# Loads moved between two DMA queues in one stage, and transfers cut by columns instead of by partitions in another

## The chip, the cores and the metric

The kernel runs on one core of a Trainium2 chip. The metric is the device time of one execution in microseconds (us). The engines are TensorE (PE in the profile, PEld for its weight loads), VectorE (DVE), ScalarE (ACT), GpSimd (POOL) and SyncE (SP). SP and POOL each issue DMA transfers in the order of their programs: an instruction that waits for a semaphore holds back everything behind it on that engine.

## The reference

Two transformer-like layers on x of 2 x 4096 tokens with 256 features, all in float32. Only the first attention of the first layer is touched by the change:

```python
h = layernorm(x) * (1 + ca) + sa
q, k, v = ...                       # 16 heads of 16; q and k normalised
def step(state, (q_t, k_t, v_t, a_t, b_t)):
    state = a_t * state
    delta = b_t * (v_t - state @ k_t)
    state = state + outer(delta, k_t)
    return state, state @ q_t       # one output per token
out = rms_norm(outs) * rms_w * silu(h @ Wgate)
x = x + ga * (out @ Wout)
```

The later parts (a token-choice feed-forward of 32 experts, a windowed attention, a mixture of 8 experts) are the same before and after.

## The kernel before

The recurrence is computed in chunks of 16 tokens. Three stages stand in a row, each with its own block of instructions for every engine and a barrier at its end.

**Chunk stage** (`build_delta_chunks`). 64 tiles of 128 tokens go through a software pipeline of 102 iterations. Phase A projects a tile and stores `rows` (v, k, q, gate), `small` and the products of pairs of tokens (`pairs_q`, `pairs_k`) to HBM. Phase B takes a group of 16 tiles, spread over 16 iterations: it reads the pairs back as two tiles `kk` and `qkd` of 128 partitions x 4096 numbers, one partition for each chunk (16 KB in a row), weighs them with decays, inverts the triangular systems in `kk` on DVE (`eliminate`), and stores the results as `inverse` and `qkd`. Phase C reads `inverse` back tile by tile (`load_inverse`), with `c_rows` and `c_fac`, ACT makes `blocks` of it, PE solves, and `vw` is stored. There are four groups. Each load and each store of `kk` and `qkd` goes in `PIECES = 4` pieces of 512 KB; piece i holds the partitions 32 i to 32 i + 31 (`lines_of`). Since a tile of tokens is 8 partitions of the group, four tiles of a group lie in one piece, and `load_inverse` waits for the one piece that holds its tile (`inverse_out[piece]`). SP issues all loads, POOL all stores.

**State scan** (`build_state_scan`): untouched.

**Output stage** (`build_delta_outputs`). 32 pairs of tiles. For pair m PE multiplies `u` by blocks (`mix`, L1300), DVE adds `read` (`add`, L1402), ACT squares, DVE reduces, ACT takes the root, DVE normalises and multiplies by the gate (L1419, signal `o_ready`), PE turns (L1310) and projects (L1319), and DVE adds the result to x (`add_x`, L1427, signal `x_ready`), from where POOL stores it as `x1`. In iteration m of DVE's program stand `add(m)`, `normalize(m)` and `add_x(m - 2)`, in that order; ACT's iteration m ends, where m % 4 is 1, with `silu(m // 4 + 1)` of the gate rows of the next four pairs. PE's order is `mix(m)`, `turn(m - 1)`, `project(m - 2)`. Buffers: two `u` of a pair (256 KB), two `read`, `qkd` and `x` of four tiles (512 KB), two `gate` of eight tiles (1 MB). All loads are SP's, in one order: `load_qkd`, `load_u`, `load_read`, and behind them at every fourth pair `load_gate` (waits for `o_ready` of the pair that last read the buffer) and at every second `load_x` (waits until the store of the buffer's old x has landed).

Of the kernel before, what the change touches and what calls it, by code (L numbers as in the profile page):

```python
# [10 lines left out]
BATCH, SEQ, DIM = 2, 4096, 256  # L11
# [83 lines left out]
def chunk_rows(dram, g):  # L95

    return dram.rearrange("(g p t) f -> g p (t f)", g=GROUPS, p=P)[bass.ds(g, 1)].rearrange("a p f -> (a p) f")
# [152 lines left out]
def build_delta_chunks(nc, d, gamma_last):  # L250
# [6 lines left out]
    PIECES = 4  # L257
    LINES = P // PIECES
    C_ROWS, C_SMALL, OUTS = 8, 4, 4
# [4 lines left out]
    with ExitStack() as ctx:  # L264
# [65 lines left out]
        fac_out, qkd_out = map(sem.from_zero, ("fac_out", "qkd_out"))  # L330
        inverse_out = [sem.from_zero(f"inverse_out{piece}") for piece in range(PIECES)]
        c_in = [sem(f"c_in{i}") for i in range(C_ROWS)]
# [4 lines left out]

        def lines_of(piece):
            return slice(piece * LINES, (piece + 1) * LINES)

# [6 lines left out]
        with nc.Block() as block:  # L347
            @block.sync
            def _(sync):
# [11 lines left out]
                def load_keys(g, piece):  # L361
                    if piece == 0:
                        for i in both:
                            sync.wait_ge(pairs_out[i], 32 * TILES_OF_GROUP // 4 * (g + 1))
                        if g > 0:
                            for out_of in inverse_out:
                                sync.wait_ge(out_of, 16 * g)
                    sync.dma_start(kk[lines_of(piece), :], chunk_rows(d["pairs_k"], g)[lines_of(piece), :]).then_inc(kk_in, 16)

                def load_queries(g, piece):  # L370
                    if piece == 0 and g > 0:
                        sync.wait_ge(qkd_out, 16 * PIECES * g)
                    sync.dma_start(qkd[lines_of(piece), :], chunk_rows(d["pairs_q"], g)[lines_of(piece), :]).then_inc(qkd_in, 16)

# [9 lines left out]
                def load_inverse(c):  # L384
                    g, m = divmod(c, TILES_OF_GROUP)
                    if c >= C_SMALL:
                        sync.wait_ge(blocks_ready, at(c - C_SMALL + 1))
                    sync.wait_ge(inverse_out[m * PIECES // TILES_OF_GROUP], 16 * (g + 1))
                    sync.dma_start(inverse[c % C_SMALL][:, :, :].rearrange("p h t -> p (h t)"), tile_rows(d["inverse"], c)).then_inc(inverse_in[c % C_SMALL], 16)
# [32 lines left out]
            def _(pool):  # L422
# [13 lines left out]
                for n in range(ITERATIONS):  # L436
# [8 lines left out]
                    if m == TILES_OF_GROUP - 3:  # L445
                        pool.wait_ge(solved, at(g + 1))
                        for piece in range(PIECES):
                            pool.dma_start(chunk_rows(d["inverse"], g)[lines_of(piece), :], kk[lines_of(piece), :]).then_inc(inverse_out[piece], 16)
                    for piece in range(PIECES):
                        g, m = group_at(n - piece)  # L450
                        if m == TILES_OF_GROUP - 1:
                            pool.wait_ge(qkd_ready, at(g + 1))
                            pool.dma_start(chunk_rows(d["qkd"], g)[lines_of(piece), :], qkd[lines_of(piece), :]).then_inc(qkd_out, 16)
                    c = n - C_LAG - 1
# [722 lines left out]
def build_delta_outputs(nc, d):  # L1177
# [5 lines left out]
    BATCH_PAIRS = PAIRS_OF_TILES // BATCH  # L1183
    EIGHTS = TILES // 8
    with ExitStack() as ctx:
        sb = lambda name, shape: ctx.enter_context(nc.sbuf_tensor("do_" + name, shape, F32))
# [12 lines left out]
        gate = [sb(f"gate{i}", [P, 8, DIM]) for i in both]  # L1199
        x = [sb(f"x{i}", [P, Q, DIM]) for i in both]  # L1200
        o = [sb(f"o{i}", [P, 2, DIM]) for i in both]
# [9 lines left out]
        turned, oT_ready, projected, x_ready, begun = map(sem, ("turned", "oT_ready", "projected", "x_ready", "begun"))  # L1211
        u_in, qkd_in, read_in, gate_in, x_in = ([sem(f"{n}{i}") for i in both] for n in ("u_in", "qkd_in", "read_in", "gate_in", "x_in"))
        x_out = [sem.from_zero(f"x_out{i}") for i in both]
        CONSTS = 16 * (3 + BATCH)
# [10 lines left out]
        with nc.Block() as block:  # L1225
            @block.sync
            def _(sync):
# [14 lines left out]

                def load_gate(e):
                    if e >= 2:
                        sync.wait_ge(o_ready, at((e - 1) * 4))
                    sync.dma_start(gate[e % 2][:, :, :], tiles_of(d["rows"], e, 8)[:, :, 3 * DIM:4 * DIM]).then_inc(gate_in[e % 2], 16)

                def load_x(q):
                    if q >= 2:
                        sync.wait_ge(x_out[q % 2], q // 2 * 16)  # L1250
                    sync.dma_start(x[q % 2][:, :, :], tiles_of(d["x"], q, Q)).then_inc(x_in[q % 2], 16)

                sync.dma_start(parity[:, :], d["parity"]).then_inc(parity_in, 16)
# [3 lines left out]
                load_read(0)  # L1257
                load_gate(0)
                sync.dma_start(w_out[:, :, :], d["w_out"].rearrange("(k p) n -> p k n", p=P)).then_inc(consts, 16)
# [5 lines left out]
                load_read(1)  # L1265
                load_x(0)
                load_x(1)
                load_gate(1)
                for m in range(2, PAIRS_OF_TILES):
                    if m % 2 == 0 and m // 2 + 1 < QUADS:  # L1270
                        load_qkd(m // 2 + 1)
                    load_u(m)
                    if m % 2 == 1 and m // 2 + 1 < QUADS:
                        load_read(m // 2 + 1)
                    if m % 4 == 3 and m // 4 + 2 < EIGHTS:
                        load_gate(m // 4 + 2)
                    if m % 2 == 1 and m >= 5 and m // 2 < QUADS:
                        load_x(m // 2)

            @block.gpsimd  # L1280
            def _(pool):
                for q in range(QUADS):
                    pool.wait_ge(x_ready, at((q + 1) * 2))
                    pool.dma_start(tiles_of(d["x1"], q, Q), x[q % 2][:, :, :]).then_inc(x_out[q % 2], 16)
                for i in both:
                    pool.wait_ge(x_out[i], QUADS // 2 * 16)

# [50 lines left out]
            def _(act):  # L1338
# [20 lines left out]
                def silu(e):  # L1359
                    act.wait_ge(gate_in[e % 2], at((e // 2 + 1) * 16))  # L1360
                    act.activation(gate[e % 2][:, :, :], gate[e % 2][:, :, :], ACT.Silu).then_inc(silued, 1)
# [23 lines left out]
            def _(vec):  # L1385
# [35 lines left out]
                def add_x(m):  # L1421
                    q, half = divmod(m, 2)
                    vec.wait_ge(projected, at(m + 1))
                    if half == 0:
                        vec.wait_ge(x_in[q % 2], at((q // 2 + 1) * 16))
                    rows = flat_pair(x[q % 2], half)
                    vec.tensor_tensor(rows, rows, y_ps[m % 2][:, :, :].rearrange("p n f -> p (n f)"), ALU.add).then_inc(x_ready, 1)  # L1427
# [1594 lines left out]
```

## Time and profile before

| | us |
|---|---|
| median of 3 runs (3786.72 to 3790.21) | 3787.32 |
| the profiled execution | 3794.78 |
| its span, first to last instruction | 3793.0 |
| chunk stage in it, about 40 to 778 | 738 |
| output stage in it, about 1309 to 1620 | 311 |

The profile is of one execution. The profiled execution's own time is 1.8 us above its span and 7.5 us above the median. Times in the rows below count from the first instruction of the span. Because the stages are separated by barriers, time that a stage loses or gains moves all later stages by the same amount.

### The profile page before, as it was taken

The page shows a single profiled execution, that of the slowest core. Times are in us where ns is not written, and L with a number is a line of the kernel's source. Part 1 is how long each engine was busy: PE and PEld are TensorE (multiplying, and loading weights), DVE is VectorE, ACT ScalarE, POOL GpSimd, SP SyncE. Part 2 cuts the span into 40 slices and gives each one's busy share as a digit, 9 for nine tenths or more (in the row PEclk, how much of TensorE's full clock was granted, in tenths as well). Part 3 has the DMA queues.
Part 4 walks back from the last instruction along what each step waited for, and adds up shares of the span by engine and source line. Part 5 has one row for each costly group of instructions (what it writes and reads, how often), then busy time and mean ns, then how long its engine had stood idle before and what let it go on. Part 6 is the DMA issues. An engine that isn't in the chain of part 4 may idle for free. (4 is left out here: it accounts for less than half of the span.)

```text
span 3793.0 us, 108279 instructions
## 1 busy us (share of the span) xinstructions
PE 2521.0 (66%) x42132; PEld 1857.3 (49%) x42132; DVE 2027.5 (53%) x5459; ACT 1309.6 (35%) x3125; POOL 791.6 (21%) x1161
## 2 busy tenths in 40 slices
PE   5987883468888565755762887777760049999900
PEld 2554553445555354622441565555540049999800
DVE  2386887646666343464023677766763024444476
ACT  3766663346666433331000343333330012222200
POOL 0222221125555400000000110010103630000076
PEclk8998995555555577776765888888865579999955
DMA  3458888834444454524957211111114322222275
GB/s 105 162 183 257 263 277 275 275 101 102 100 100 103 104 161 146 174 99 164 414 232 285 97 59 58 58 58 58 58 46 145 105 79 69 72 69 71 64 224 162
DMA packets 387346, 534.51 MB, mean 141 GB/s; under 512 B 122140, under 2 KB 315640, under 8 KB 379384
## 3 DMA queue, kind: packets, MB, share of 16 engines
q1 hardware_dynamic: 308184, 343.88, 28.4%
q0 software_dynamic: 58688, 152.42, 12.8%
q10 hardware_dynamic: 20320, 36.44, 2.6%
q8 instruction: 61, 1.00, 0.1%
q14 instruction: 93, 0.76, 0.1%
HBM read 327.58 MB, written 216.15 MB: 143 GB/s over the span
## 5 line engine op out<-in xcount | busy, mean ns | idle before, releaser
L1108 ACT ACTIVATE ss_write_ps<-ss_state,ss_gammas 128x64 f32<-128x64 f32 x1024 | 263.3, 303 | 196.9 <-DVE ss_state L1156 196.9
L479 PE MATMUL dc_rows_ps<-dc_weights,dc_hT 128*128 128x512 f32 x512 | 264.0, 640 | 20.0 <-ACT dc_rows L608 17.4
L2728 PE MATMUL se_up_ps<-se_xT,se_w 128*128 128x128 f32 x2176 | 266.3, 276 | 0.1
L2736 PE MATMUL se_y_ps<-se_w,se_aT 128*128 128x256 f32 x1088 | 257.2, 379 | 0.0
L2728 PEld LDWEIGHTS se_up_ps<-se_xT,se_w 128*128 128x128 f32 x2176 | 254.8, 193 | 0.5 <-DVE se_w L2793 0.5
L2866 POOL DMA_INDIRECT cb_y<-scratch_ys,cb_to x128 | 137.3, 1073 | 564.1 <-DVE cb_to L2880 525.4
L2793 DVE COPY se_w<-mx_weights 128x2048 f32 x136 | 166.7, 1227 | 101.5 <-issue 101.5
L2736 PEld LDWEIGHTS se_y_ps<-se_w,se_aT 128*128 128x128 f32 x1088 | 196.4, 190 | 21.1
L1073 PE MATMUL ss_write_ps<-ss_solved,ss_k_rows 16*64 16x64 f32 x4096 | 180.7, 322 | 38.2 <-DVE ss_solved L1151 37.9
L1156 DVE TENSOR_TENSOR ss_state<-ss_write_ps,ss_block_mask 128x128 f32<-128x128 f32 x512 | 129.5, 291 | 135.7 <-PE ss_write_ps L1073 135.7
L2718 PE MATMUL se_xt_ps<-se_ident,se_xs 128*128 128x128 f32 x272 | 52.2, 275 | 223.0 <-DMA se_xs<-scratch_xs 223.0
L2763 ACT COPY se_xT<-se_xt_ps 128x256 f32<-128x256 f32 x136 | 50.6, 372 | 412.8 <-PE se_xt_ps L2718 412.8
L1030 POOL DMA_DIRECT2D scratch_solved_u<-ss_solved x256 | 135.4, 529 | 251.5 <-DVE ss_solved L1151 229.5
L1064 PE MATMUL ss_read_ps<-ss_state,ss_wq 128*32 128x64 f32 x4096 | 168.0, 314 | 26.3 <-DVE ss_state L1156 25.3
L1073 PEld LDWEIGHTS ss_write_ps<-ss_solved,ss_k_rows 16*64 16x64 f32 x4096 | 136.7, 208 | 93.9 <-ACT ss_write_ps L1108 62.0
L2799 DVE COPY se_y<-se_y_ps 128x256 f32<-128x256 f32 x136 | 57.7, 424 | 214.6 <-PE se_y_ps L2736 214.6
L1300 PE MATMUL do_mix_ps<-do_u,do_blocks 32*32 32x16 f32 x8192 | 89.0, 189 | 121.0 <-DMA do_u<-scratch_solved_u 73.5
L2288 POOL TENSOR_TENSOR wa_exps<-wa_exps,wa_nears 128x192 f32<-128x192 f32 x64 | 38.7, 605 | 594.9 <-ACT wa_one L2233 594.9
L2647 POOL DMA_INDIRECT scratch_xs<-dp_h,dp_to x128 | 125.8, 983 | 140.1 <-issue 115.6
L2718 PEld LDWEIGHTS se_xt_ps<-se_ident,se_xs 128*128 128x128 f32 x272 | 38.3, 142 | 238.1 <-DMA se_ident<-in_ident 224.5
L1300 PEld LDWEIGHTS do_mix_ps<-do_u,do_blocks 32*32 32x32 f32 x8192 | 85.2, 118 | 133.8 <-issue 133.8
L2768 ACT ACTIVATE se_aT<-se_up_ps 128x512 f32<-128x512 f32 x136 | 81.2, 597 | 196.2 <-PE se_up_ps L2728 196.2
(350 smaller groups left out, 5762.0 us busy)
## 6 DMA issues: line engine op xcount, KB each, us to landing
ex_w<-in_w_all SPq DMA_DIRECT2D x64, 1024.0 KB, 21.1
scratch_rows<-dc_rows POOLq DMA_DIRECT2D x64, 512.0 KB, 6.2
scratch_vw<-dc_out POOLq DMA_DIRECT2D x64, 512.0 KB, 6.7
dc_c_rows<-scratch_rows SPq DMA_DIRECT2D x64, 384.0 KB, 6.1
scratch_xs<-wa_zeros ACTq DMA_DIRECT2D x34, 512.0 KB, 14.6
se_xs<-scratch_xs SPq DMA_DIRECT2D x136, 128.0 KB, 2.0
scratch_ys<-se_y SPq DMA_DIRECT2D x136, 128.0 KB, 1.7
ss_wq_rows<-scratch_vw SPq DMA_DIRECT2D x128, 128.0 KB, 2.3
```

The source lines that it names most:

```text
L479: mm = pe.matmul(to, hT[i][:, k, :], weights[:, k, columns], start=(k == 0), stop=(k == HALVES - 1), skip_group_check=True)
L1030: pool.dma_start(to, solved[i][lines, b, :, :]).then_inc(out_done[i], 16)
L1064: mm = pe.matmul(read_ps[b][u * QUAD:(u + 1) * QUAD, 0:WIDTH], wq[i][:, b, u, c, :], state[b][:, k, :], start=True, stop=True, skip_group_ ...
L1073: mm = pe.matmul(write_ps[b][side_of(u), k, 0:WIDTH], k_rows[i][rows_of(u), b, c, :], solved[i][rows_of(u), b, c, :], start=False, stop=Tr ...
L1108: ins = act.activation(write_ps[b][:, k, 0:WIDTH], state[b][:, k, :], ACT.Copy, scale=gammas[i][:, b, k, c:c + 1])
L1156: vec.tensor_tensor(state[b][:, :, :], write_ps[b][:, :, 0:WIDTH], block_mask[:, :].unsqueeze(1).broadcast_to([P, HALVES, WIDTH]), ALU.mul ...
L1300: mm = pe.matmul(mix_ps[i][tokens, n, h * HEAD:(h + 1) * HEAD], blocks[i][tokens, n, h, :, :].rearrange("p c t -> p (c t)"), u[i][tokens, ...
L2647: pool.indirect_dma_start(d["xs"], bass.IndirectOffsetOnAxis(ap=to[i][k * NT + j][:, :], axis=0), h[i][:, j, :], None, bounds_check=SLOTS ...
L2728: mm = pe.matmul(up_ps[i % 2][:, c * P:(c + 1) * P], w[i % (2 * AHEAD)][:, k * DFF + c * P:k * DFF + (c + 1) * P], xT[i % 2][:, k, :], sta ...
L2736: mm = pe.matmul(y_ps[i % 2][:, 0:DIM], aT[i % 2][:, c, :], w[i % (2 * AHEAD)][:, HALVES * DFF + c * DIM:HALVES * DFF + (c + 1) * DIM], st ...
L2793: vec.tensor_copy(w[i % (2 * AHEAD)][:, :], weights[:, bass.ds(expert, 1), :].rearrange("p a f -> p (a f)")).then_inc(w_ready, 1)
L2866: pool.indirect_dma_start(y[i][:, k * NT + j, :], None, d["ys"], bass.IndirectOffsetOnAxis(ap=to[i][k * NT + j][:, :], axis=0), bounds_che ...
```

## The change

In the output stage x gets four buffers (`XS = 4`), and the loads of x and of the gate rows go from SP's queue to POOL's, where the stores of x1 are. POOL first issues two gate loads and four x loads. Then, for each q of 16, it waits for `x_ready` of both pairs of q, stores x1, issues for odd q the gate load q // 2 + 2, and for q >= 1 the x load q + 3. In the chunk stage a piece of a bulk transfer is now a quarter of the columns of all 128 partitions (4 KB of each), not 32 whole partitions; the four semaphores `inverse_out` become one, and `load_inverse` waits for all four pieces of its group.

```diff
-    LINES = P // PIECES
+    PART = PAIRS // PIECES
...
-        inverse_out = [sem.from_zero(f"inverse_out{piece}") for piece in range(PIECES)]
+        inverse_out = sem.from_zero("inverse_out")
...
-        def lines_of(piece):
-            return slice(piece * LINES, (piece + 1) * LINES)
+        def part(rows, piece):
+            return rows[:, piece * PART:(piece + 1) * PART]
...
-                            for out_of in inverse_out:
-                                sync.wait_ge(out_of, 16 * g)
-                    sync.dma_start(kk[lines_of(piece), :], chunk_rows(d["pairs_k"], g)[lines_of(piece), :]).then_inc(kk_in, 16)
+                            sync.wait_ge(inverse_out, 16 * PIECES * g)
+                    sync.dma_start(part(kk, piece), part(chunk_rows(d["pairs_k"], g), piece)).then_inc(kk_in, 16)
...
-                    sync.dma_start(qkd[lines_of(piece), :], chunk_rows(d["pairs_q"], g)[lines_of(piece), :]).then_inc(qkd_in, 16)
+                    sync.dma_start(part(qkd, piece), part(chunk_rows(d["pairs_q"], g), piece)).then_inc(qkd_in, 16)
...
-                    sync.wait_ge(inverse_out[m * PIECES // TILES_OF_GROUP], 16 * (g + 1))
+                    sync.wait_ge(inverse_out, 16 * PIECES * (c // TILES_OF_GROUP + 1))
...
-                            pool.dma_start(chunk_rows(d["inverse"], g)[lines_of(piece), :], kk[lines_of(piece), :]).then_inc(inverse_out[piece], 16)
+                            pool.dma_start(part(chunk_rows(d["inverse"], g), piece), part(kk, piece)).then_inc(inverse_out, 16)
...
-                            pool.dma_start(chunk_rows(d["qkd"], g)[lines_of(piece), :], qkd[lines_of(piece), :]).then_inc(qkd_out, 16)
+                            pool.dma_start(part(chunk_rows(d["qkd"], g), piece), part(qkd, piece)).then_inc(qkd_out, 16)
...
+    XS = 4
...
-        x = [sb(f"x{i}", [P, Q, DIM]) for i in both]
+        x = [sb(f"x{i}", [P, Q, DIM]) for i in range(XS)]
...
-                load_gate(0)
...
-                load_x(0)
-                load_x(1)
-                load_gate(1)
...
-                    if m % 4 == 3 and m // 4 + 2 < EIGHTS:
-                        load_gate(m // 4 + 2)
-                    if m % 2 == 1 and m >= 5 and m // 2 < QUADS:
-                        load_x(m // 2)
...
             def _(pool):
+                def load_gate(e):
+                    if e >= 2:
+                        pool.wait_ge(o_ready, at((e - 1) * 4))
+                    pool.dma_start(gate[e % 2][:, :, :], tiles_of(d["rows"], e, 8)[:, :, 3 * DIM:4 * DIM]).then_inc(gate_in[e % 2], 16)
+
+                def load_x(q):
+                    if q >= XS:
+                        pool.wait_ge(x_out[q % XS], q // XS * 16)
+                    pool.dma_start(x[q % XS][:, :, :], tiles_of(d["x"], q, Q)).then_inc(x_in[q % XS], 16)
+
+                load_gate(0)
+                load_gate(1)
+                for q in range(XS):
+                    load_x(q)
                 for q in range(QUADS):
                     pool.wait_ge(x_ready, at((q + 1) * 2))
-                    pool.dma_start(tiles_of(d["x1"], q, Q), x[q % 2][:, :, :]).then_inc(x_out[q % 2], 16)
-                for i in both:
-                    pool.wait_ge(x_out[i], QUADS // 2 * 16)
+                    pool.dma_start(tiles_of(d["x1"], q, Q), x[q % XS][:, :, :]).then_inc(x_out[q % XS], 16)
+                    if q % 2 == 1 and q // 2 + 2 < EIGHTS:
+                        load_gate(q // 2 + 2)
+                    if q >= 1 and q - 1 + XS < QUADS:
+                        load_x(q - 1 + XS)
+                for i in range(XS):
+                    pool.wait_ge(x_out[i], QUADS // XS * 16)
```

## Rows read from the trace of the kernel before

**Rows 1.** Busy time by stretch: the columns, then chunk stage, output stage, two stretches.

```profile
core 0: us, PE busy (x) PEld busy (x) DVE busy (x) ACT busy (x) POOL busy (x), PEclk, DMA share, GB/s
40.00:778.00 738.00, 530.04 (x17544) 351.87 (x17544) 494.53 (x889) 403.61 (x857) 168.23 (x292) 0.82 0.72 230
...
289.00:299.00 10.00, 8.79 (x159) 5.14 (x157) 8.04 (x11) 5.74 (x12) 4.28 (x8) 1.00 1.02 214
...
1309.00:1620.00 311.00, 188.78 (x8576) 163.32 (x8576) 125.39 (x228) 117.62 (x184) 12.07 (x16) 0.72 0.51 165
...
1430.00:1440.00 10.00, 0.00 (x0) 0.00 (x0) 0.75 (x2) 0.02 (x1) 0.75 (x1) 0.60 0.85 282
```

**Rows 2.** Waits in the output stage: total us, times, longest.

```profile
PE do_mix_ps L1300 <- DMA do_u<-scratch_solved_u: 73.5, 7, 12.6
```

**Rows 3.** Waits of SP's queue in the output stage: total, times, longest.

```profile
SPq L1246 <- DVE do_o L1419: 100.9, 6, 21.7
...
SPq L1251 <- DMA scratch_x<-do_x: 52.6, 9, 9.1
```

**Rows 4.** Timeline, DVE's `add` of pairs 3, 9, 10, 11, 18, 27.

```profile
1351.44 0.69 DVE L1402 TENSOR_TENSOR do_o<-do_mix_ps,do_read 128x512 f32<-128x512 f32 x1 [1.53 <-PE do_mix_ps L1300]
...
1413.87 0.69 DVE L1402 TENSOR_TENSOR do_o<-do_mix_ps,do_read 128x512 f32<-128x512 f32 x1 [1.61 <-PE do_mix_ps L1300]
1418.78 0.68 DVE L1402 TENSOR_TENSOR do_o<-do_mix_ps,do_read 128x512 f32<-128x512 f32 x1
1425.77 0.68 DVE L1402 TENSOR_TENSOR do_o<-do_mix_ps,do_read 128x512 f32<-128x512 f32 x1
...
1498.16 0.69 DVE L1402 TENSOR_TENSOR do_o<-do_mix_ps,do_read 128x512 f32<-128x512 f32 x1 [3.93 <-PE do_mix_ps L1300]
...
1583.35 0.68 DVE L1402 TENSOR_TENSOR do_o<-do_mix_ps,do_read 128x512 f32<-128x512 f32 x1
```

**Rows 5.** Timeline of one period of four pairs, other engines (PE, DVE, ACT, POOL).

```profile
1418.15 1.28 ACT L1361 ACT_TABLE_LOAD   x1
1418.18 0.68 DVE L1427 TENSOR_TENSOR do_x<-do_x,do_y_ps 128x512 f32<-128x512 f32 x1
...
1419.16 0.75 POOL L1284 DMA_DIRECT2D scratch_x<-do_x  x1 [25.20 <-DVE do_x L1427]
1419.44 1.91 ACT L1361 ACTIVATE do_gate<-do_gate 128x2048 f32<-128x2048 f32 x1
...
1425.31 1.11 PE L1310 MATMUL do_tr_ps<-do_ident,do_o 128*128 128x128 f32 x4 [2.19 <-DVE do_o L1419]
...
1426.21 3.08 PE L1319 MATMUL do_y_ps<-do_w_gated,do_oT 128*128 128x256 f32 x8
...
1523.47 3.61 PE L1300 MATMUL do_mix_ps<-do_u,do_blocks 32*32 32x16 f32 x256 [12.09 <-DMA do_u<-scratch_solved_u]
```

**Rows 6.** DMA issues: count, KB each, median us from issue to landing.

```profile
dc_x<-in_x SPq DMA_DIRECT2D x16, 512.0 KB, 6.1
...
dc_kk<-scratch_pairs_k SPq DMA_DIRECT2D x16, 512.0 KB, 10.1
...
do_gate<-scratch_rows SPq DMA_DIRECT2D x8, 1024.0 KB, 5.5
```

**Rows 7.** Timeline of the chunk stage at a group's inverse stores (POOL, SP, ACT, DVE).

```profile
288.22 1.97 POOL L448 DMA_DIRECT2D scratch_inverse<-dc_kk  x4 [1.82 <-DVE dc_kk L866]
...
292.46 0.32 SPq L389 DMA_DIRECT2D dc_inverse<-scratch_inverse  x1
292.83 2.15 SPq L353 DMA_DIRECT2D dc_x<-in_x  x1
...
303.50 0.58 ACT L608 COPY dc_rows<-dc_rows_ps 128x512 f32<-128x512 f32 x1 [6.99 <-issue]
...
309.10 1.41 DVE L196 BATCH_NORM_STATS2 dc_stats<-dc_x 128x6 f32<-128x256 f32 x4 [5.81 <-DMA dc_x<-in_x]
...
710.00 0.91 ACT L654 ACTIVATE dc_blocks<-dc_inverse,dc_parity 128x256 f32<-128x256 f32 x2 [12.03 <-DMA dc_inverse<-scratch_inverse]
```

More of the change, by code:

```diff
@@ L384, in load_inverse @@
                 def load_inverse(c):
-                    g, m = divmod(c, TILES_OF_GROUP)
                     if c >= C_SMALL:
                         sync.wait_ge(blocks_ready, at(c - C_SMALL + 1))
-                    sync.wait_ge(inverse_out[m * PIECES // TILES_OF_GROUP], 16 * (g + 1))
+                    sync.wait_ge(inverse_out, 16 * PIECES * (c // TILES_OF_GROUP + 1))
                     sync.dma_start(inverse[c % C_SMALL][:, :, :].rearrange("p h t -> p (h t)"), tile_rows(d["inverse"], c)).then_inc(inverse_in[c % C_SMALL], 16)
@@ L1211, in build_delta_outputs @@
         turned, oT_ready, projected, x_ready, begun = map(sem, ("turned", "oT_ready", "projected", "x_ready", "begun"))
-        u_in, qkd_in, read_in, gate_in, x_in = ([sem(f"{n}{i}") for i in both] for n in ("u_in", "qkd_in", "read_in", "gate_in", "x_in"))
-        x_out = [sem.from_zero(f"x_out{i}") for i in both]
+        u_in, qkd_in, read_in = ([sem(f"{n}{i}") for i in both] for n in ("u_in", "qkd_in", "read_in"))
+        gate_in = [sem.from_zero(f"gate_in{i}") for i in both]
+        x_in, x_out = ([sem.from_zero(f"{n}{i}") for i in range(XS)] for n in ("x_in", "x_out"))
         CONSTS = 16 * (3 + BATCH)
@@ L1241, in load_read @@
                     sync.dma_start(read[q % 2][:, :, :], tiles_of(d["solved_q"], q, Q)).then_inc(read_in[q % 2], 16)
[L1243 to L1251, printed above, removed]
                 sync.dma_start(parity[:, :], d["parity"]).then_inc(parity_in, 16)
@@ L1359, in silu @@
                 def silu(e):
-                    act.wait_ge(gate_in[e % 2], at((e // 2 + 1) * 16))
+                    act.wait_ge(gate_in[e % 2], (e // 2 + 1) * 16)
                     act.activation(gate[e % 2][:, :, :], gate[e % 2][:, :, :], ACT.Silu).then_inc(silued, 1)
@@ L1424, in add_x @@
                     if half == 0:
-                        vec.wait_ge(x_in[q % 2], at((q // 2 + 1) * 16))
-                    rows = flat_pair(x[q % 2], half)
+                        vec.wait_ge(x_in[q % XS], (q // XS + 1) * 16)
+                    rows = flat_pair(x[q % XS], half)
                     vec.tensor_tensor(rows, rows, y_ps[m % 2][:, :, :].rearrange("p n f -> p (n f)"), ALU.add).then_inc(x_ready, 1)
```

## The prediction

> **What bounds the kernel now.** I read the busy time by stretch first, for the two stages that the diff touches. No engine is full in either. In the output stage TensorE is busy 189 of 311 us, VectorE 125, and the DMA engines half of the time; in the chunk stage VectorE is busy 495 of 738 us and the DMA engines 72% [rows 1]. So in both stages something waits, and I looked for what waits last.
>
> Output stage: the waits say that PE stands before `mix` for u seven times, 73.5 us in all [rows 2]. SP's own waits tell why u is late: SP, which also issues u, stands 100.9 us before the gate load, until DVE has multiplied by the old gate, and 52.6 us before x loads, until an x store has landed [rows 3]. Nothing behind these waits is issued, u least of all. DVE's timeline shows the effect: the adds of pairs 9, 10, 11 come 4.91 and 6.99 us apart, the fed pace, and PE then idles 12 us before the next period's first mix [rows 4, 5]. From pair 3 to pair 27, six periods of four pairs, it takes 1583.35 - 1351.44 = 231.9 us, or 38.7 a period [rows 4].
>
> Chunk stage: at a group's inverse stores the DMA engines are full (share 1.02) yet move only 214 GB/s, whereas the output stage's 1 KB runs over all partitions move 282 at a share of 0.85, or 332 for a full one [rows 1]. Meanwhile others wait: ACT 6.99 us for buffers whose stores stand behind these pieces, DVE 5.81 us for an x load that took from 292.83 to 309.10, 16 us [rows 7], where the median is 6.1 [rows 6]. In the last group ACT waits 12.03 us for its first inverse tile [rows 7].
>
> **The change, output stage.** Taken off SP: the gate and x waits. What is left before u on SP are waits for blocks and sums that PE's own mix two pairs back also implies, so u is issued at once and I count no stall for it (at the other end all of the 73.5 us stays, which is the fourth rival below). That frees the fed pace: 4.9 us a pair, 7.0 for the pair behind a silu, which is the interval from pair 10 to 11 [rows 4]; the silu itself is a table load of 1.28 and 1.91 us [rows 5].
>
> But what is late next is the gate. POOL issues gate e behind the x1 store of pairs 4e-6 and 4e-5, which waits for `add_x(4e-5)`. DVE does that at the end of iteration 4e-3, and ACT wants the gate at the end of that same iteration 4e-3. In the rows iteration 4e-3 is the one whose add starts at 1413.87: its `add_x` ends at 1418.86, the store is issued from 1419.16 to 1419.91 and the gate could be issued 6.05 us after the add; ACT's silu begins at 1419.44, 5.57 after the add [rows 4, 5]. So even a load that landed at once would be 0.5 us late. Landing: 5.5 us is the median of SP's gate loads [rows 6], and the store of 512 KB just ahead adds something under 1.5, so I take 6.15 and the gate at 12.2: a stall of 12.2 - 5.57 = 6.6 us for each of e = 2 to 7. Bounds: 0.5 (landed at once) and 6.05 + 10.1 - 5.57 = 10.6 (landing like the kk pieces, the slowest row of its kind) [rows 6]. Behind the waiting silu on ACT stand square and root of pair 4e-2, and DVE's reduce waits for these; nothing covers it.
>
> The stall also lets PE go slow. After only 2.2 us idle its turn took 1.11 and ended, with the projection, 3.98 us after its start, and after 12 us idle the mix took 3.61 us [rows 5] (granted clock 0.60 in such an idle stretch, where 0.5 is the lower level of 1.2 GHz [rows 1]); at that speed turn, projection and mix take 7.6 where DVE needs 4.9 a pair. PE starts about 0.45 us before DVE's add [rows 4, 5], so the next interval is 7.2. A period is then 4.9 + (7.0 + 6.6) + 7.2 + 4.9 = 30.6. Pairs 17 to 19 carry about 6.5 us more now, PE waiting inside the mix as at 1498.16 [rows 4]; I keep it. Six periods: 183.6 + 6.5 = 190, against 231.9: minus 42.
>
> The start gets dearer: POOL's two gate and four x loads, 4.2 MB, come at once beside SP's first qkd and u. At 332 GB/s they fill 12.6 us [rows 1]. If SP's go first the cost is nothing, if POOL's go first 12.6; I take 5, below the middle, because the old SP stream also had 3 MB of these loads ahead of the second round. x itself: its load is issued some five pairs ahead, 25 us against a landing near 6 [rows 6], so it costs nothing; without that cover it would cost what the gate does. The extra POOL instructions are 0.75 us each on an engine that is busy 12 of 311 us [rows 1, 5]. Output stage: -42 + 5 = **-37 us**.
>
> The Trainium skill ("DMA: Bandwidth & Descriptors", Rules for kernel authors) says that spreading DMAs over SP, ACT and GpSimd does not help bandwidth, since all run on the same 16 engines, and only saves issue time. By that alone the stage would gain nothing. The DMA share of 0.51 [rows 1] says that bandwidth isn't what it lacks; the rule is a rival below.
>
> **Chunk stage.** 64 pieces of 512 KB are 33.5 MB. At 214 GB/s they hold the DMA engines 157 us, at 332 GB/s 101 [rows 1]: 56 us less, 14 in each group. How much of it is on the path? A group's inverse stores (2.1 MB, 9.8 us before, 6.3 after) lie on it in all four groups, by the waits above: 3.5 x 4 = 14. The kk loads and qkd stores that follow save 0.88 each, 8 pieces in four groups, 28; I count half, because DVE and PE also limit there. The qkd loads lie where DMA has room: nothing, and with that cover gone another 14. Against this stands the new wait. SP now issues the first inverse tile when all four pieces have landed, not the first: before, 4.2 us after the stores' issue [rows 7]; now about 2 + 6.3, so 4 us later. Behind it on SP stand an x load, `load_group` and the kk loads. The x load took 16 us because it ran beside the stores [rows 7], so waiting them out costs it nothing; in the last group, where ACT waits for the tile itself, I charge the 4. Sum: -14 - 14 + 4 = **-24 us**. Bounds: -56 (everything on the path) and +16 (no faster, and 4 us in each group).
>
> The Trainium skill ("SBUF — State Buffer", Door 1: The DMA port swizzle) has partitions 0 to 31 reach 8 of 16 ports, 189 GB/s against 328 at 1 MiB. By these figures the pieces would save, as an estimate from that page, 75 us of DMA time and not 56. The row's 214 holds some stores over all partitions too, so the two don't contradict.
>
> **Sum.** -37 - 24 = -61 against the profiled 3794.78, which gives 3734; that execution is 7.5 us above the median of the runs, so the forecast is 3787.3 - 61 = **3726 us**.
>
> **Rivals.** *Gate not late in effect*, ACT finding cover: takes away 6 x (6.6 + 2.3) = 53, 3673. Against it speaks the program's order, which makes it late by 0.5 at least. *All of the DMA time on the path*: -56 in place of -24, 3694; for it, the engines full at every group's change. *The chunk stage gains nothing or pays the wait*: 0 to +16, so 3750 to 3766; for it, VectorE and PE, busy 67% and 72% of the stage [rows 1]. *Spreading the queues doesn't help* (the rule of the Trainium skill quoted above): the order of queues isn't what counts, output stage unchanged, 3763; against it stand SP's waits [rows 3]. *Slower*: the gate load, beside u, qkd, read and x in flight, takes the 16 us that the x load took beside the stores [rows 7]. The stall becomes 6.05 + 16.3 - 5.57 = 16.8, 10.2 more in each of six, 61 us: with the chunk stage as forecast, 3787; with its 0 to +16, 3811 to 3827. It decides from a landing of 16 us on.
>
> **How the numbers follow.** Forecast 0.46 (own range 3700 to 3750: stall 3 to 10, chunk stage -10 to -40); gate not late 0.08; all DMA time 0.14; chunk stage nothing 0.16; spreading no help 0.06; late gate, slower or even, 0.10. From 3678 to 3768 all but the last and most of the first rival are held. The first five are faster by over 0.2% (7.6 us, about what a measurement of this kernel can tell from no change): 0.90; the last is halved, 0.05 within 0.2% and 0.05 slower.
>
> **What would show it.** SP's waits before gate and x are gone, and PE's waits for u with them. ACT shows six waits of about 6.6 us for `do_gate`, in pairs 5, 9 and so on to 25; from pair 3 to 27 about 190 us pass. The first add comes about 5 us later after the stage's start. kk pieces land well below 10.1 us and the stretch of the inverse stores moves some 330 GB/s. Wrong would be: gate waits over 10 us, PE still waiting for u, or SP's wait for the inverse longer than 10 us with ACT idle behind it.

## The result and the profile after

The changed kernel takes 3718.66 us, median of 4 runs (3710.95 to 3724.49), beside 3787.02 of the kernel before on the same chip: ratio 0.9815 [0.98, 0.983], or 68.4 us less. The profiled execution took 3720.33 us, its span 3718.6. Of the three stages of this attention only the two that the diff touches changed. By the first load of each next stage, the chunk stage ends at 739.70 us, where it ended at 778.70; from the output stage's first load to its last x1 store it takes 273.1 us, where it took 306.0. The state scan between them takes 530.3, where it took 531.1.

Busy time by stretch of the changed kernel (columns as in [rows 1]): the chunk stage, its first inverse stores, the output stage.

```profile
40.00:739.00 699.00, 527.16 (x17544) 353.87 (x17544) 493.72 (x889) 404.47 (x857) 169.24 (x292) 0.83 0.69 242
286.50:293.00 6.50, 6.50 (x179) 3.96 (x179) 2.60 (x7) 5.04 (x11) 2.19 (x5) 1.00 0.91 352
1270.00:1543.00 273.00, 178.89 (x8576) 153.73 (x8576) 125.07 (x228) 117.51 (x184) 30.47 (x39) 0.74 0.58 186
```

The busy times of PE and DVE are nearly those of [rows 1]; what went is time in which they waited. Waits of the output stage after (total us, times, longest), first of the engines, then of SP's queue:

```profile
ACT do_gate L1361 <- DMA do_gate<-scratch_rows: 55.4, 7, 9.7
```

```profile
SPq L1231 <- PE do_mix_ps L1300: 102.9, 23, 10.3
SPq L1241 <- DVE do_o L1402: 65.4, 14, 12.7
SPq L1236 <- ACT do_blocks L1345: 40.3, 13, 3.2
```

SP's waits before gate and x [rows 3] are gone, and of PE's waits for u [rows 2] none is left in this stretch. What SP waits for now are buffers that PE, DVE and ACT have just used, and after the start no engine waits for the loads behind it. In their place ACT waits for the gate. One period of four pairs, from the timeline of all engines:

```profile
1355.86 0.68 DVE L1402 TENSOR_TENSOR do_o<-do_mix_ps,do_read 128x512 f32<-128x512 f32 x1
...
1360.13 1.28 ACT L1361 ACT_TABLE_LOAD   x1
...
1360.76 0.68 DVE L1402 TENSOR_TENSOR do_o<-do_mix_ps,do_read 128x512 f32<-128x512 f32 x1
...
1361.14 0.76 POOL L1280 DMA_DIRECT2D scratch_x<-do_x  x1 [10.03 <-DVE do_x L1427]
1361.89 0.89 POOL L1267 DMA_DIRECT2D do_gate<-scratch_rows  x1
...
1370.29 1.91 ACT L1361 ACTIVATE do_gate<-do_gate 128x2048 f32<-128x2048 f32 x1 [8.88 <-DMA do_gate<-scratch_rows]
...
1372.75 0.69 DVE L1408 TENSOR_REDUCE do_rms<-do_squares 128x32 f32<-128x512 f32 x1 [11.30 <-ACT do_squares L1353]
...
1376.15 1.12 PE L1310 MATMUL do_tr_ps<-do_ident,do_o 128*128 128x128 f32 x4 [11.14 <-DVE do_o L1419]
...
1376.61 0.68 DVE L1402 TENSOR_TENSOR do_o<-do_mix_ps,do_read 128x512 f32<-128x512 f32 x1
1377.06 3.21 PE L1319 MATMUL do_y_ps<-do_w_gated,do_oT 128*128 128x256 f32 x8
...
1380.20 2.33 PE L1300 MATMUL do_mix_ps<-do_u,do_blocks 32*32 32x16 f32 x256
...
1382.58 0.69 DVE L1402 TENSOR_TENSOR do_o<-do_mix_ps,do_read 128x512 f32<-128x512 f32 x1 [1.00 <-PE do_mix_ps L1300]
```

The period repeats the one of [rows 5] with another wait in it. POOL issues the gate load 6.03 us after the add of pair 9, ACT wants it 5.55 after (table load done at 1361.41), and it lands only at 1370.29. ACT stands 8.88 us, then DVE for 11.30, and the add of pair 11 comes 15.85 us after that of pair 10. Six such gate waits last 8.85 to 9.71 us.

Landing times of the changed kernel (count, KB each, median us):

```profile
dc_kk<-scratch_pairs_k SPq DMA_DIRECT2D x16, 512.0 KB, 8.8
...
scratch_inverse<-dc_kk POOLq DMA_DIRECT2D x16, 512.0 KB, 4.6
...
scratch_qkd<-dc_qkd POOLq DMA_DIRECT2D x16, 512.0 KB, 8.2
...
do_gate<-scratch_rows POOLq DMA_DIRECT2D x8, 1024.0 KB, 8.7
```

The kk pieces land in 8.8 us in place of 10.1, the gate in 8.7 from POOL in place of 5.5 from SP [rows 6]. Timeline of the changed chunk stage at the stores that stood in [rows 7]:

```profile
286.04 2.12 POOL L446 DMA_DIRECT2D scratch_inverse<-dc_kk  x4 [1.82 <-DVE dc_kk L864]
293.15 0.32 SPq L387 DMA_DIRECT2D dc_inverse<-scratch_inverse  x1
293.52 0.60 SPq L353 DMA_DIRECT2D dc_x<-in_x  x1
```

and ACT's first tile of the last group:

```profile
675.98 0.91 ACT L652 ACTIVATE dc_blocks<-dc_inverse,dc_parity 128x256 f32<-128x256 f32 x2 [7.49 <-DMA dc_inverse<-scratch_inverse]
```

SP issues the first tile 7.1 us after the stores' issue, where it took 4.2, because it waits for all four pieces; yet ACT's wait in the last group is 7.49 us in place of 12.03 [rows 7]. The stores now move 352 GB/s where the stretch before showed 214 [rows 1]. The Trainium skill ("SBUF — State Buffer", Door 1: The DMA port swizzle) has 32 partitions reach half of the ports and measures 189 GB/s for them against 328 for all, at 1 MiB. In size this trace agrees, with 214 and 352. But the ports themselves are seen in no run here, and the change also cuts a row from 16 KB to 4 KB; no run separates the number of partitions from the length of the rows.

### The profile page after: what moved, and what is told of

It is laid out like the page before. It is cut to its first block and busy times, and to the rows that moved or that the text cites. A ratio compares the mean times of both kernels' runs of the same rounds, so it can differ in the third digit from the quotient of the medians.

```text
span 3718.6 us, 108270 instructions
## 1 busy us (share of the span) xinstructions
PE 2512.0 (68%) x42132; PEld 1852.5 (50%) x42132; DVE 2027.9 (55%) x5459; ACT 1311.2 (35%) x3125; POOL 812.3 (22%) x1185
## 5 line engine op out<-in xcount | busy, mean ns | idle before, releaser
L2736 PEld LDWEIGHTS se_y_ps<-se_w,se_aT 128*128 128x128 f32 x1088 | 196.4, 190 | 21.1
L2288 POOL TENSOR_TENSOR wa_exps<-wa_exps,wa_nears 128x192 f32<-128x192 f32 x64 | 38.1, 596 | 594.9 <-ACT wa_one L2233 594.9
L1062 PEld LDWEIGHTS ss_read_ps<-ss_state,ss_wq 128*32 128x32 f32 x4096 | 105.0, 150 | 81.0 <-DVE ss_state L1154 77.4
L1149 DVE TENSOR_TENSOR ss_solved<-ss_u_rows,ss_read_ps 128x64 f32<-128x64 f32 x512 | 107.8, 221 | 61.3 <-PE ss_read_ps L1062 51.7
## 6 DMA issues: line engine op xcount, KB each, us to landing
ex_w<-in_w_all SPq DMA_DIRECT2D x64, 1024.0 KB, 21.1
```

The source lines that it names most:

```text
L1062: mm = pe.matmul(read_ps[b][u * QUAD:(u + 1) * QUAD, 0:WIDTH], wq[i][:, b, u, c, :], state[b][:, k, :], start=True, stop=True, skip_group_ ...
L1149: vec.tensor_tensor(solved[i][:, b, c, :], u_rows[i][:, b, c, :], read_ps[b][:, 0:WIDTH], ALU.subtract).then_inc(u_ready[b], 1)
L2736: mm = pe.matmul(y_ps[i % 2][:, 0:DIM], aT[i % 2][:, c, :], w[i % (2 * AHEAD)][:, HALVES * DFF + c * DIM:HALVES * DFF + (c + 1) * DIM], st ...
```

## The experiments

**The two parts alone.** The lines of the diff in `build_delta_outputs` are applied to the kernel before, and in another kernel those in `build_delta_chunks`.

Expected of the output stage's part: 

> The output stage's part alone, chunk stage as before. If the two parts add up, the output stage gains the 33 us that it gained in the changed kernel (306 to 273 us from its first load to its last store) and the chunk stage none: about 3754 us. Rival: part of the output stage's gain hung on where the chunk stage left the chip (clock, queues); then under 25 us, and the two parts alone don't sum to 68.

Measured: 3751.20 us, ratio 0.9907 [0.9888, 0.9926], 36 us less.

Expected of the chunk stage's part: 

> The chunk stage's part alone, output stage as before. If the parts add up, 39 us less: about 3748 us, with the stage ending at about 740 us in place of 779. Rival, the forecast's own sum: 24 us, 3763.

Measured: 3750.64 us, ratio 0.9905 [0.9889, 0.9922], 37 us less. Together the parts give 73 where the whole gave 68 to 70, within what the intervals allow: they are nearly independent, and about equal.

**Is it the late gate?** In the changed kernel the gate load is moved ahead of the wait for `x_ready` and of the x1 store on POOL:

```diff
                 for q in range(QUADS):
+                    if q % 2 == 1 and q // 2 + 2 < EIGHTS:
+                        load_gate(q // 2 + 2)
                     pool.wait_ge(x_ready, at((q + 1) * 2))
                     pool.dma_start(tiles_of(d["x1"], q, Q), x[q % XS][:, :, :]).then_inc(x_out[q % XS], 16)
-                    if q % 2 == 1 and q // 2 + 2 < EIGHTS:
-                        load_gate(q // 2 + 2)
```

Expected: 

> The changed kernel with the gate load issued on GpSimd ahead of the wait for x_ready, not behind the store. Theory of the late gate: the gate is then issued when the old one has been read, two iterations or some 9.8 us earlier, against waits of 9.2 us, so the six waits of ACT go to nearly nothing, and with them 6 x (9.2 + about 2 for the slow TensorE behind each) = 67 us at most: 3655 to 3665 us, from pair 3 to 27 some 135 to 145 us. Rival: with the gate in time something else comes due, u or read loads or TensorE at its lower clock, and no more than half comes back: about 3690. Second rival: the wait is that of a GpSimd queue that is behind in any case; then nothing changes, 3718.

Measured: 3675.85 us (3671.35 to 3677.57), ratio 0.9701 [0.9685, 0.9718], 43 us below the changed kernel. The gate waits are gone, though a gate load lands no faster. Waits, then landing, of this kernel:

```profile
ACT do_gate L1361 <- DMA do_gate<-scratch_rows: 0.6, 1, 0.6
```

```profile
do_gate<-scratch_rows POOLq DMA_DIRECT2D x8, 1024.0 KB, 9.1
```

From pair 3 to 27 it takes 151.4 us against 199.3 in the changed kernel. So the wait for the gate is what the stage paid. It missed the expected 3655 to 3665 for two reasons. At the fed pace of [rows 4] six periods would take 130.1 us, and 21.3 came on top. Some 8.4 of them are at pairs 18 and 19 (10.72 and 9.57 us in place of 4.9 and 7.0), where PE pauses inside the mix and no stall covers the pauses any more. The other 12.9 are at the pairs behind the six silus and at pair 17 behind one of these, because the silu itself still stops TensorE; the timeline behind one:

```profile
1359.82 1.11 PE L1310 MATMUL do_tr_ps<-do_ident,do_o 128*128 128x128 f32 x4 [1.82 <-DVE do_o L1419]
...
1360.73 3.62 PE L1319 MATMUL do_y_ps<-do_w_gated,do_oT 128*128 128x256 f32 x8
...
1364.28 2.87 PE L1300 MATMUL do_mix_ps<-do_u,do_blocks 32*32 32x16 f32 x256
```

After 1.82 us idle, turn, projection and mix take 7.3 us, and the next add comes 6.93 us after the last one and not 4.90. The granted clock was 1.00 from 1352 to 1358 us and 0.66 on average from 1358 to 1368; behind the next silu it stood at 0.50 from 1385 to 1395. So the slow turn and projection don't need a late gate: the short stop that the silu itself makes is enough, and they stay when the lateness goes.

**The queue, or the place in its order?** The gate loads go back to SP at their old place, and x stays in four buffers on POOL:

```diff
...
                     if m % 2 == 1 and m // 2 + 1 < QUADS:
                         load_read(m // 2 + 1)
+                    if m % 4 == 3 and m // 4 + 2 < EIGHTS:
+                        load_gate(m // 4 + 2)
...
-                load_gate(0)
-                load_gate(1)
                 for q in range(XS):
                     load_x(q)
...
-                    if q % 2 == 1 and q // 2 + 2 < EIGHTS:
-                        load_gate(q // 2 + 2)
```

Expected: 

> The changed kernel with the gate loads back on SP at their old place (behind u of every fourth pair, m % 4 = 3), x in four buffers on POOL. Theory: the gate wait on SP was the larger holder of u, so PE's waits for u come back, some 8 to 10 us in each of six periods in place of a gate stall of 9; the output stage keeps little of its gain: 3720 to 3750. Rival (the x wait was the holder, the gate wait rides on it): no wait for u and none for the gate, 3665 to 3690.

Measured: 3750.72 us (3749.25 to 3750.99), ratio 0.9903 [0.9887, 0.992]: what the chunk stage's part alone gives and just above the expected range, so the whole gain of the output stage is gone. SP's waits and PE's waits of its output stage:

```profile
SPq L1246 <- DVE do_o L1419: 98.9, 6, 20.4
```

```profile
PE do_mix_ps L1300 <- DMA do_u<-scratch_solved_u: 71.4, 6, 12.1
```

The 52.6 us of waits before x [rows 3] don't occur any more, and beside the gate's wait they were worth nothing; the gate's wait alone holds u, as in [rows 2, 3]. What they would cost once the gate's wait is gone was not tested: no kernel has the gate in a better place and x on SP. Then the same kernel with the gate load two pairs later in SP's order:

```diff
-                    if m % 4 == 3 and m // 4 + 2 < EIGHTS:
-                        load_gate(m // 4 + 2)
+                    if m % 4 == 1 and 2 <= m // 4 + 1 < EIGHTS:
+                        load_gate(m // 4 + 1)
```

Expected: 

> The changed kernel with the gate loads on SP, but two pairs later in its order (behind u of the pair at whose end ACT wants the next gate rows, m % 4 = 1), where DVE has already multiplied by the old gate, so that SP stands less; x stays on POOL. Theory (the place in the order counts, not the queue): neither gate nor u is waited for, about as the variant with the gate ahead of the x1 store, 3670 to 3685. Rival (it must be another queue): the gate wait on SP holds u again, 3715 or more.

Measured: 3683.26 us (3680.84 to 3689.97), ratio 0.9732 [0.9716, 0.9748]. SP's wait there:

```profile
SPq L1246 <- DVE do_o L1419: 19.8, 6, 3.4
```

PE's waits for u come down from 71.4 us to 19.0, in five waits, so u is still held a little. One place in SP's own order gives 67 of the 75 us that lie between the variant with the gate on SP at its old place and the one with the gate early on POOL. The Trainium skill ("DMA: Bandwidth & Descriptors", Rules for kernel authors) says that spreading DMAs over issuing engines does not help bandwidth. These runs agree in so far as the gate needed no second queue (x had left SP in all of them). What the move to POOL changed is who stands behind whose wait.

**The size of the stall.** Gate on SP, but released by the event behind which POOL issues it in the changed kernel:

```diff
                 def load_gate(e):
                     if e >= 2:
-                        sync.wait_ge(o_ready, at((e - 1) * 4))
+                        sync.wait_ge(x_ready, at((e - 1) * 4))
...
-                    if m % 4 == 1 and 2 <= m // 4 + 1 < EIGHTS:
+                    if m % 4 == 2 and 2 <= m // 4 + 1 < EIGHTS:
```

(against the kernel just above). Expected: 

> The changed kernel, with the gate loads on SP but released by the same event as in the changed kernel (add_x of pair 4e-5, whose store POOL issues first there), behind u of pair 4e-2. Theory: the size of the stall is that event plus the landing, and a gate load lands in 8.7 us from POOL and in 5.4 from SP; the stall shrinks from 9.2 to some 5.5 us, the time by 6 x 3 to 4 = 18 to 24 us, to 3695 to 3701. Rival (the landing depends on the x and u transfers beside it, not on the queue): unchanged, about 3718. Rival (the wait on SP holds the next u): 3725 or more.

Measured: 3699.94 us (3697.53 to 3701.42), ratio 0.9775 [0.9758, 0.9791], 15 us below the changed kernel by the ratios and 19 by the medians. ACT's waits between 1300 and 1530 us, total, times, longest:

```profile
ACT do_gate L1361 <- DMA do_gate<-scratch_rows: 33.4, 6, 5.7
```

5.6 us each in place of 9.2. The stall is that event plus the issue and the landing. Of the 3.6 us that it lost, 2.6 are the landing (on average 6.1 us from SP, 8.7 from POOL) and 1.0 the issue, which comes 5.00 us after the add and not 6.03, because SP does not issue the x1 store first. PE's waits for u did come back (32.5 us, six), but inside the stall: in five of the six periods the add behind the silu comes 12.3 to 12.6 us after the one before, which is 7.0 and 5.6.

**The start.** To the variant with the early gate, a wait is added on POOL between the first gate load and the five others of the burst:

```diff
                 load_gate(0)
+                pool.wait_ge(summed, at(1))
                 load_gate(1)
```

Expected: 

> The variant with the gate loads ahead of the x1 store (3676), where POOL at the stage's start issues the first gate load alone and waits for the first add before it issues the second gate load and the four x loads. Theory (the first read and u loads share the DMA engines with this burst, and the first add comes 5 us later for it): 5 us less, about 3671, with the first add some 14 us after the stage's start as before the change. Rival (it is SP's own loads that limit the start, or the x loads come too late now): 3676 to 3685.

Measured: 3672.68 us (3670.0 to 3674.07), ratio 0.9703 [0.9686, 0.9719]; the variant without the wait had 0.9701 beside its own runs of the kernel before. No gain shows, though the intervals of the two ratios would hide 5 us; the trace decides. DVE's first two adds (the stage's first load is at 1268.49):

```profile
1282.85 0.69 DVE L1403 TENSOR_TENSOR do_o<-do_mix_ps,do_read 128x512 f32<-128x512 f32 x1 [32.35 <-PE do_mix_ps L1301]
1296.54 0.69 DVE L1403 TENSOR_TENSOR do_o<-do_mix_ps,do_read 128x512 f32<-128x512 f32 x1 [8.17 <-PE do_mix_ps L1301]
```

and PE's timeline over the same time:

```profile
1274.57 2.42 PE L1301 MATMUL do_mix_ps<-do_u,do_blocks 32*32 32x16 f32 x164 [24.43 <-DMA do_u<-scratch_solved_u]
1281.35 1.91 PE L1301 MATMUL do_mix_ps<-do_u,do_blocks 32*32 32x16 f32 x128 [4.35 <-issue]
1288.29 1.91 PE L1301 MATMUL do_mix_ps<-do_u,do_blocks 32*32 32x16 f32 x128 [5.04 <-issue]
1295.04 1.46 PE L1301 MATMUL do_mix_ps<-do_u,do_blocks 32*32 32x16 f32 x92 [4.84 <-issue]
```

The first add does come 4.6 us earlier (14.36 us after the stage's start, against 18.99 in the variant without the wait), but the second one not: 28.05 against 28.20. Before the second PE stands three times for "issue", 14.2 us, whatever the loads do. The burst's delay is hidden behind these.

**The parts of the chunk stage**, each on the kernel before. The inverse stores by columns, with the wait for all four:

```diff
-                            pool.dma_start(chunk_rows(d["inverse"], g)[lines_of(piece), :], kk[lines_of(piece), :]).then_inc(inverse_out[piece], 16)
+                            pool.dma_start(part(chunk_rows(d["inverse"], g), piece), part(kk, piece)).then_inc(inverse_out[piece], 16)
```

Expected: 

> The kernel before with only the inverse stores cut by columns, and the wait for all four pieces that this needs. The forecast's term: 14 us for the stores less 4 for the wait, so 10 us less, 3777. Rival: the stores are the main thing, because x, rows and small transfers all stood beside or behind them at each group's change; then 25 us or more, about 3760. Third: the wait for all pieces eats the gain, no change, 3787.

Measured: 3769.44 us, ratio 0.9952 [0.9935, 0.9968], 18 us less. The wait alone (pieces as before):

```diff
-                    sync.wait_ge(inverse_out[m * PIECES // TILES_OF_GROUP], 16 * (g + 1))
+                    for out_of in inverse_out:
+                        sync.wait_ge(out_of, 16 * (g + 1))
```

Expected: 

> The kernel before, with only the wait changed: the load of an inverse tile waits for all four pieces of its group, and the pieces stay 32 partitions each. Forecast's term for the wait: 4 us in the last group, up to 16 in four, so 3791 to 3803. Rival (the wait is dear, and faster stores hide it in the changed kernel): every group's first tile comes a whole set of stores later, 10 us x 4, so about 3820. Rival (nothing waits for the tile): 3787.

Measured: 3786.27 us over 10 runs, ratio 0.9999 [0.999, 1.0009]. Nothing, although ACT's first tile of the last group does come late:

```profile
713.81 0.91 ACT L655 ACTIVATE dc_blocks<-dc_inverse,dc_parity 128x256 f32<-128x256 f32 x2 [21.78 <-DMA dc_inverse<-scratch_inverse]
```

The row at 710.00 of [rows 7] is only 3.8 us earlier, but this execution was 5.9 us ahead when it issued the group's stores (688.93 against 694.86). Counted from there the first tile is 9.7 us later, since four slow pieces are waited for. The fifth tile comes 37.5 us after the stores' issue (726.42), where it came 37.2 in the kernel before (732.08): the lateness is made up. Everything but the inverse stores by columns:

```diff
-                    sync.dma_start(kk[lines_of(piece), :], chunk_rows(d["pairs_k"], g)[lines_of(piece), :]).then_inc(kk_in, 16)
+                    sync.dma_start(part(kk, piece), part(chunk_rows(d["pairs_k"], g), piece)).then_inc(kk_in, 16)
...
-                    sync.dma_start(qkd[lines_of(piece), :], chunk_rows(d["pairs_q"], g)[lines_of(piece), :]).then_inc(qkd_in, 16)
+                    sync.dma_start(part(qkd, piece), part(chunk_rows(d["pairs_q"], g), piece)).then_inc(qkd_in, 16)
...
-                            pool.dma_start(chunk_rows(d["qkd"], g)[lines_of(piece), :], qkd[lines_of(piece), :]).then_inc(qkd_out, 16)
+                            pool.dma_start(part(chunk_rows(d["qkd"], g), piece), part(qkd, piece)).then_inc(qkd_out, 16)
```

Expected: 

> The kernel before, with the kk and qkd loads and the qkd stores by columns, and the inverse stores still by 32 partitions with a wait for one piece. If the gains add up, this gives what the columns of the inverse stores (-18) left of the whole chunk stage's part (-37): -19, so 3768. The forecast's own term for it is -14, 3773. Rival (the stores of the inverse were all that counted, and the two runs shared no gain by accident): 3787. Rival (the transfers overlap, so either part alone lets go of the same wait): below 3760.

Measured: 3772.03 us, ratio 0.9955 [0.9941, 0.9969], 16 us less. Of these edits the first two, the loads, alone:

Expected: 

> The kernel before, with the kk and qkd loads alone by columns; inverse and qkd stores stay by 32 partitions. All transfers but the inverse stores gave -16. The forecast's view, half of the kk loads and of the qkd stores and nothing for the qkd loads: the kk part of 14 is 7, 3780. Rival (the loads carry all of it, since eliminate waits for kk): 3771. Rival (the qkd stores carry it): 3787.

Measured: 3782.81 us over 10 runs, ratio 0.9989 [0.998, 0.9999], 3 to 4 us less. And the third, the qkd stores, alone:

Expected: 

> The kernel before, with the qkd stores alone by columns. All transfers but the inverse stores gave -16, the loads of kk and qkd among them -3. If gains add up, the qkd stores carry the rest, -13: 3774. Forecast's term for them (half of 0.88 for each piece): -7, 3780. Rival (only loads and stores together help): 3784 to 3787.

Measured: 3776.56 us over 12 runs, ratio 0.9973 [0.9963, 0.9984], 10 us less by the ratio. The parts add up within what the intervals allow: stores of the inverse 18, stores of qkd 10, loads 4, wait 0, so 32 against 37 for all. Most of it is in the stores. By which wait they count stays open. ACT's wait for its inverse tiles over the stage falls with the gains, from 58.1 us in the kernel before to 54.6 with the loads alone by columns, 45.5 with the qkd stores, 43.6 with the inverse stores, 40.6 with all but these and 38.1 with all. But with the wait alone it rises to 72.3, and the time stays. Nor did the qkd stores, alone by columns, land faster in the profiled execution (11.2 us against 11.3).

## Why the prediction was right, and which terms were mis-sized

The forecast was 3726 us and the range 3678 to 3768; 3718.66 lies 7 below the one and inside the other. The mechanisms were the ones named, each seen in the profile: u freed, the gate late, the stores faster. Sizes were off in both directions and partly cancelled: the output stage was put at -37 and gave -36 alone (-33 in the profile of the whole), the chunk stage at -24 and gave -37. That the output stage came so near is luck, as its terms show.

**Output stage, six periods:** forecast 190 us from pair 3 to 27, measured 1512.65 - 1313.37 = 199.3 in the changed kernel and 191.8 in the output part alone. Two terms were wrong. The stall is 9.2 us, not 6.6, because the landing was taken at 6.15 from SP's gate loads, and POOL's six take 8.4 to 9.2; issue at 6.03 and need at 5.55 after the add were as forecast to 0.02 us. That is 2.6 x 6, some 15.5 us too little. Against it stand two terms that were put too high. The intervals behind the stalls were to be 7.2 in all six periods, 43.2; pair 4 has no stall ahead of it (4.9), and the five others took 6.0, 6.6, 6.7 and twice 7.7, together 39.5. In the period shown above this is because the mix behind the slow projection took 2.33 us and not 3.61. And the 6.5 us that pairs 17 to 19 pay for PE's pauses inside the mix are no extra: the adds of pairs 18 and 19 came 10.36 and 10.67 us after the ones before, 21.0, where an add of 4.9 and one of 16.2 with the stall make 21.1. The stall covers them. In the changed kernel alone pairs 17 and 25 took 2.0 us more each. Sum: 190 + 15.5 - 3.7 - 6.5 + 4.0 = 199.3. In the output part alone the intervals behind the stalls sum to 36.0, so 13.7 too high stand against 15.5 too low, and its 191.8 lies near 190 by luck. The output part alone took 5.6 to 5.8 us at pairs 16 and 24 and 4.9 at 17 and 25. The granted clock tells them apart: 0.50 through pairs 16 and 24 and 0.65 in the pairs behind in the changed kernel, 0.76 to 0.79 and then 1.00 in the output part alone. Why it rose later in one execution than in the other stays open.

**The start:** forecast +5, first add measured +4.8, but by pair 3 only +1.7 (43.4 us after the stage's first load, against 41.6). The step failed in that it let a late first add be a late stage: the next adds wait for PE's own pauses, which the shorter burst showed. These pauses, three before pair 1, add up to 12.8 us in the kernel before (4.51, 3.95, 4.29) and to 14.7 in the changed one (4.80, 5.04, 4.84), and that is the 1.9 us by which the add of pair 1 is later behind the start of the first mix.

**Freed u at no stall:** held, no wait for u after the start. The fourth rival (spreading the queues doesn't help) falls in its result, 36 us gained, though the gate needed only another place in SP's order. The rival that ACT finds cover falls as well: the gate is late, by the program's order. The slower rival needed a landing of 16 us and got 8.7.

**Chunk stage:** forecast -24, measured -37. The inverse stores were put at -14 and gave -18 (interval -12 to -25) with their wait; the wait itself was put at +4 and costs 0 (within 4), because a late first tile is made up four tiles later; kk loads and qkd stores were put at -7 each and gave -4 and -10. The term for the inverse stores was too small because a group's four pieces were put at 9.8 us before and 6.3 after; from the first issue to the last landing they took 13.4 to 14.1 and 7.1 to 8.8, 24 less in four groups where 14 was counted. The miss of 13 is then 4 for the wait, 4 for the inverse stores, 3 for the qkd stores, minus 3 for the loads, and 5 that the parts don't show alone; each of these is near what a single run of this kind can tell. "Half of it, because DVE and PE also limit" was too careful for stores and too generous for loads. The rival "all of the DMA time, -56" was wrong in the other direction.

**The best version** of those run has the gate load early: 3675.85 us, or 3672.68 with the shorter burst, which cannot be told apart. The first is 43 us faster than the changed kernel and differs from it by the place of one load in POOL's order.

## What to carry to other kernels

When a load with a late release is moved out of a shared queue, ask what stands before it in the new one: here some 75 us were to be had by no longer holding u (3750.64 against 3675.85), and 43 of them were lost by standing behind a store that is released at the moment the load is needed. Price a moved transfer by the landing time of the queue that it goes to, not of the one it leaves. Of transfers cut by partitions, try the stores first: here they gave 28 us, those whose result is read back in the same stage 18 of them, and the loads 4. And a delay ahead of a wait that exists anyway (a late first add before PE's pauses, a late first tile before a surplus of later ones) costs nothing, so test it before it is charged.

## What the runs showed of the hardware

The same 1 MB gate load lands in a median of 8.6 to 9.2 us in the four kernels in which POOL issues it and in 5.3 to 6.2 where SP does; released by the same wait, it is 9.1 in the variant at 3676 and 5.3 in the one at 3683. x loads of 512 KB took 3.9 to 8.2 us from SP behind the first two, 5.3 in the median. In the changed kernel, behind the burst, those that POOL issues right behind a gate load take 9.2 to 10.1, the others 5.7 to 6.6, so what else stands in POOL's queue counts too; what makes the gate itself slower there was not separated. I had counted a transfer's time as the same from either queue. The pieces of the inverse, 512 KB each, land in 4.6 us stored by columns where pieces of 32 partitions took 7.4, while the kk loads gained less (8.8 against 10.1). And at the output stage's start PE's small matmuls pause three times for 3.2 to 5.0 us with "issue" as the only cause the profile names, which hid 5 us of late data. The pauses stand behind the 164th, 292nd and 420th of these matmuls in all 14 kernels, 128 apart, and more of them, of 1.1 to 4.6 us, behind the 4733rd and 4861st, where PE's second loop begins. So they belong to a place in PE's program, not to the data; why they come there is not shown.
